# Block numbers side by side in DRAM, and tiles that travel on all 128 partitions, in a graph-network kernel

## The reference

```python
msg  = concat([h[src], h[dst]]) @ WM + bM            # one row per edge, 64 wide
s, mean_sq, mx, mn = sum, mean of squares, max, min of msg over the edges into each node
agg  = concat([mean, mx, mn, std, var, s])
hu   = concat([h, agg, agg * amp, agg * att]) @ WU + bU
hbn  = batchnorm(hu / sqrt(n))
out  = leaky_relu(hbn @ Wmix + bmix) + h
h    = relu(batchnorm(out)) + h
```

## Time and profile before

| what | value |
|---|---|
| median of three runs | 3956.39 us |
| the profiled execution, its span on the core | 3968.1 us |
| TensorE / VectorE / GpSimd busy | 84% / 79% / 56% of the span |
| DMA moved | 668.65 MB in 300094 packets |
| SP's queue (q1) | 188676 packets, 35.4% of 16 engines' span |
| fetches of numbers, keeps, fetches of one-hots | 130, 130, 395, of 593.1 KB each |

### The profile page before, as it was taken

One profiled execution on the slowest core, in us unless ns is written; L12 is line 12 of the kernel. 1 busy time (PEld: TensorE's weight loads), 2 busy tenths in 40 slices (PEclk: granted clock), 3 DMA queues, 4 the chain that ended last, 5 costly groups with the idle time before them and its releaser, 6 DMA issues.

```text
span 3968.1 us, 88783 instructions
## 1 busy us (share of the span) xinstructions
PE 3314.0 (84%) x29640; PEld 2061.9 (52%) x29640; DVE 3137.6 (79%) x6027; ACT 1168.6 (29%) x3428; POOL 2223.3 (56%) x2221
## 2 busy tenths in 40 slices
PE   0055699898887799999998699999988799999986
PEld 0022344444446657555558456555557466655575
DVE  6598588788776778888877678888876788888876
ACT  4302122222223612222225322222225332222243
POOL 6402577666654037777753147777750177777640
PEclk9997899999998899999999899999999899999997
DMA  7003799889896056556672256566670366566750
GB/s 209 16 0 81 217 257 258 239 247 254 248 258 210 14 163 178 175 173 191 201 232 77 79 157 178 170 175 191 198 240 16 118 174 180 170 189 189 219 163 34
DMA packets 300094, 668.65 MB, mean 169 GB/s; under 512 B 81751, under 2 KB 180237, under 8 KB 296995
## 3 DMA queue, kind: packets, MB, share of 16 engines
q1 hardware_dynamic: 188676, 419.32, 35.4%
q0 software_dynamic: 78400, 192.26, 18.5%
q10 hardware_dynamic: 32732, 54.15, 3.9%
HBM read 517.78 MB, written 151.72 MB: 169 GB/s over the span
## 4 chain that ended last, share of the span: by engine, by line
PE 21%; issue 20%; DMA 18%; DVE 12%; POOL 12%; ACT 2%; SPq 1%; DVEq 1%; ACTq 0%; POOLq 0%
POOL rows L881 11%; DMA rows<-table,lists 10%; PE bank L1815 8%; DMA RE<-vd 6%; PE bank L1789 4%; PE bank L1882 4%; DVE accL L1438 2%; DVE scr L1361 2%; PE bank L1798 2%; DVE scr L1372 1%; DVE accL L1434 1%; PE bank L1870 1%; DMA RE<-ohd 1%; DMA left<-accL 1%; SPq L476 1%
## 5 line engine op out<-in xcount | busy, mean ns | idle before, releaser
L881 POOL DMA_INDIRECT rows<-table,lists x1828 | 1833.0, 1003 | 836.6 <-issue 518.1
L1815 PE MATMUL bank<-RE,split 125*64 125x482 bf16 x15600 | 1846.5, 370 | 18.9 <-ACT scr L605 18.9
L1815 PEld LDWEIGHTS bank<-RE,split 125*64 125x64 bf16 x15600 | 948.9, 111 | 691.0 <-issue 34.2
L632 ACT ACTIVATE split<-rows,masks 128x128 f32<-128x128 f32 x1828 | 600.1, 391 | 1693.5 <-DMA rows<-table,lists 1311.9
L1789 PE MATMUL bank<-RE,split 126*64 126x482 bf16 x7800 | 924.2, 372 | 79.8 <-DVE scr L1372 60.4
L1361 DVE TENSOR_TENSOR scr<-scr,bank 128x964 f32<-128x964 f32 x624 | 692.1, 1109 | 78.8 <-PE bank L1789 74.0
L1372 DVE TENSOR_TENSOR scr<-scr,bank 128x964 f32<-128x964 f32 x624 | 692.0, 1109 | 45.0 <-PE bank L1798 40.0
L1789 PEld LDWEIGHTS bank<-RE,split 126*64 126x64 bf16 x7800 | 471.6, 111 | 430.5 <-DVE scr L1372 67.1
L1798 PE MATMUL bank<-RE,flip_w 126*64 126x482 bf16 x2600 | 391.4, 373 | 112.8 <-DVE scr L1361 69.0
L1433 DVE TENSOR_TENSOR accL<-accL,rows 128x192 f32<-128x192 f32 (+2 forms) x664 | 224.6, 338 | 292.8 <-DMA rows<-table,lists 289.9
L1438 DVE TENSOR_TENSOR accL<-accL,split 128x384 f32<-128x384 f32 (+2 forms) x664 | 343.1, 517 | 1.7
(11 more groups left out here) (282 smaller groups left out, 2752.9 us busy)
## 6 DMA issues: line engine op xcount, KB each, us to landing
RE<-ohd SPq DMA_DIRECT2D x395, 593.1 KB
RE<-vd SPq DMA_DIRECT2D x130, 593.1 KB
ohd<-RE SPq DMA_DIRECT2D x130, 593.1 KB
rows<-table,lists POOLq DMA_INDIRECT x1828
left<-accL POOLq DMA_DIRECT2D x20, 1280.0 KB
dense_d<-scr ACTq DMA_DIRECT2D x104, 241.0 KB
split<-dense_d ACTq DMA_DIRECT2D x16, 625.0 KB, 6.5
table<-accL SPq DMA_DIRECT2D x36, 250.0 KB
```

The source lines that it names most:

```text
L632: ins = nc.scalar.activation(masked_rows[:, g % GM_RING * GC + k, :], ring[:, b * GC + k, :], ACT.Copy, scale=masks[:, m:m + 1])
L881: nc.gpsimd.indirect_dma_start(ring[:, b * GC + k, :], None, table, bass.IndirectOffsetOnAxis(ap=lists[:, c:c + 1], axis=0)).then_inc(col_ ...
L1815: ins = nc.tensor.matmul(SB[h * D:(h + 1) * D, 0:CH], split[0:NP, k, q, h * D:(h + 1) * D], columns_of(k, NP), start=k == 0 and q == 0, st ...
```

## The change

The numbers are copied once, DRAM to DRAM, to a new array `by_chunk` in which the 2410 numbers of a chunk and group lie side by side. A fetch of numbers then is one run of 2410 for each partition. It and the keeps, the fetches of one-hots and the compare use all 128 partitions in place of 126; `ohd` grows to 128 rows a tile. TensorE's reads (126 or 125 rows) stay as they are.

```diff
-    ohd = nc.dram_tensor("ohd", (NCH * GROUPS, NP + 1, GB), BF16).ap()
+    ohd = nc.dram_tensor("ohd", (NCH * GROUPS, P, GB), BF16).ap()
     vd = nc.dram_tensor("vd", (TILES, QP), BF16).ap()
+    by_chunk = nc.dram_tensor("by_chunk", (NCH, TILES * CH), BF16).ap()
...
             sp.wait_ge(S["vd_st"], 16 * 5)
-            numbers = vd.rearrange("(g k) q -> g k q", k=RING)
+            sp.dma_start(by_chunk.rearrange("c (k n) -> c k n", n=CH), vd.rearrange("k (c n) -> c k n", n=CH)).then_inc(S["chunked"], 16)
+            sp.wait_ge(S["chunked"], 16)
+            numbers = by_chunk.rearrange("c (g n) -> (c g) n", g=GROUPS)
...
-                sp.dma_start(VB[slot][0:NP + 1, :].rearrange("p (k n) -> p k n", k=RING),
-                             numbers[g:g + 1, :, ds(c * CH, CH)].to_broadcast([NP + 1, RING, CH])).then_inc(vb_ld[slot], 16)
+                sp.dma_start(VB[slot], numbers[ds(c * GROUPS + g, 1), :].to_broadcast([P, GB])).then_inc(vb_ld[slot], 16)
...
-                sp.dma_start(ohd[ds(g, 1), :, :].rearrange("o p n -> (o p) n"), BK[b][0:NP + 1, :]).then_inc(oh_st[b], 16)
+                sp.dma_start(ohd[ds(g, 1), :, :].rearrange("o p n -> (o p) n"), BK[b]).then_inc(oh_st[b], 16)
...
-                sp.dma_start(BK[g % STREAM][0:NP + 1, :],
+                sp.dma_start(BK[g % STREAM],
                              ohd[ds(ahead, 1), :, :].rearrange("o p n -> (o p) n")).then_inc(oh_ld[g % STREAM], 16)
...
-                    nc.vector.tensor_scalar(BK[b][0:NP + 1, :], VB[g % 2][0:NP + 1, :], answers[0:NP + 1, :], None,
+                    nc.vector.tensor_scalar(BK[b], VB[g % 2], answers, None,
                                             ALU.is_equal).then_inc(S["cmp"], 1)
```

More of the change, by code:

```diff
@@ L367, in build @@
             "codes codes_ps codes_ev hot_done ps1 ps1_used ps2 rank_done sc_pos pos_ld "
-            "e_ready e_used v_ps v_int v_low v_ev vd_st cmp "
+            "e_ready e_used v_ps v_int v_low v_ev vd_st chunked cmp "
             "big_mx big_mx2 turns_done "
```

## The result

The changed kernel takes 3895.62 us (median of 4 runs, 3876.84 to 3901.81) against 3956.26 us, a ratio of 0.9833 with a 95% interval of 0.9814 to 0.9852: 61 us faster. 3868 was forecast, in a range of 3822 to 3922. Its runs spread over 25 us, those of before over 3 us. The profiled execution has a span of 3897.3 us, 71 us less than before's 3968.1.

The account below looks back on a forecast made before the run. Layer 0's dense part was taken as bound by DMA on fourteen full engines. Middle -68, start -8, end -5, layers 1 to 3 -7 and copy 0 make -88 us: 3956.4 to 3868 us, range 3822 to 3922.

Parts of the forecast that it names:

- Fourteen full engines: Layer 0's dense part: transfers of 126 rows use 14 DMA engines, which are full; 128 rows get 16.
- The middle of layer 0: Layer 0, 560 to 1200 us: pace falls from 6.32 to 5.65 us a group, gaining 68 us, bounds 22 and 107.
- the term of 5.56 for DMA: Middle of layer 0: 5.56 us a group if all DMA-bound again, two transfers of 32.2 us on 16 engines plus 1.53.
- that of 5.26 for GpSimd: Middle of layer 0: TensorE with GpSimd limit the pace to 5.26 us a group, taken from layer 1.
- The start of layer 0: Stretch up to 560 us: gain of 8 us, bounds 0 and 20; gain ahead of the gathers' lists capped at about 9.
- The copy: Start of layer 0: the new copy of 650 pieces uses 13 engines, 3.1 us plus some 2.5 to land, hidden, cost 0.
- The end of layer 0: The last compare's 13.1 us wait for numbers shrinks: gain of 5 us, bounds 0 and 13.
- Layers 1 to 3: One-hot fetches on 16 engines instead of 14, with TensorE at 98%: 7 us gain in all, bounds 0 and 30.
- The signs: Whole launch: 144 packets a transfer, compare waits under 30 us, middle pace 5.5 to 5.8, VectorE 90% or more, later layers within 5 us each.
- One address read by 128 rows: Slower rival, fetch of numbers: repeated reads of the same 4820 bytes get dearer, middle loses 42 us, 3998 us; chance 0.06.
- The faster rival: All layers: full-width transfers also faster for each engine, 24 us a transfer, pace 5.3, -134 us, 3822 us; chance 0.16.
- The gathers take over: Middle of layer 0: VectorE's waits for gathered rows keep the pace at 6.0, 3916 us; the smaller gain's chance 0.13.

Follow-up runs that it names:

- experiment 4: The changed kernel, with GpSimd leaving out the third gather of each column group in all layers (output not the reference's): 3797.20 us, ratio 0.9592.

## Why the prediction was right, and where it was off

- **Fourteen full engines.** Right. Width and run length, taken apart, each take off 0.75 us of DMA time a group, and the packet counts show 126 + 14 and 128 + 16, and 16 + 13 in place of 5 + 5 for the cut stores. The Trainium skill's rule on the number of DMA engines (DMA: Bandwidth & Descriptors, "Why a DMA increments its semaphore by 16 and not by 1") agrees, and for 125 rows too.
- **The middle of layer 0.** 68 us were forecast. The pace came out at 5.75, not 5.65, which is 101 x 0.57 = 57 us; over the same 90 groups, from the 31st to the 121st compare, it fell from 6.27 to 5.74. The number was near partly by luck, as two errors offset each other: the term of 5.56 for DMA was too high and that of 5.26 for GpSimd too low. DMA needs 4.73, because a transfer costs 28.8 us and not 32.2, and the other queues 1.13 and not 1.53. GpSimd needs (410 + 110) / 93.9 = 5.54 us a group. I had taken its limit from layer 1's pace, but that was TensorE's: the gathers of both kernels' stretches say what GpSimd itself needs (before's layer 1 at 1450 to 2050 us, then after at 560 to 1100):

```profile
L881 POOL DMA_INDIRECT rows<-table,lists x444 | 439.2, 989 | 170.8 <-issue 124.1 <-DVE accL L1438 46.6
...
L883 POOL DMA_INDIRECT rows<-table,lists x381 | 409.1, 1074 | 130.1 <-issue 110.1 <-DVE accL L1440 20.1
```

In layer 1 it was (439.2 + 124.1) / 114 = 4.94 us a group. Layer 0 has 4.06 gathers a group instead of 3.89 (its 457 gathers start at 457 us, when 14 of the 130 groups are past their compare), and each costs 1.36 us with its issue instead of 1.27. Much of the second rise goes with the compares, which run only in layer 0: in this stretch the 136 gathers that overlap a compare take 1.22 us in the mean, the other 244 take 0.99, as layer 1's do. A longer gather is likelier to overlap one, so this is a strong sign and not a proof. The Trainium skill (SBUF — State Buffer, "Who interferes with whom") has VectorE operations of this kind in a two-port mode lock GpSimd out while it writes descriptors; the durations fit, but no run here takes the compare away.
- **The start of layer 0.** Mis-sized: 8 us forecast, 0.6 seen. The step that failed was to take the gathers' lists (cap of 9 us) for the gate. The gate was ScalarE's order of issues, which held the 24.6 us won by the 13th compare until nothing was left of them; it is visible in before's trace in the same place, and I had not read that engine's rows.
- **The copy.** Right. Issued at 346.60 and landed before the next fetch's issue at 352.45, 5.8 us (5.6 forecast); the first compare starts at 367.6 (367.3 before). Cost 0. The queue from 346 to 352.4 us shows 663 packets, which are 650 pieces and 13 closing ones, so 13 engines as forecast:

```profile
q1 hardware_dynamic: 663, 0.63, 34.8%
```

- **The end of layer 0.** The last wait for numbers fell from 13.1 us to 5.9, 7 us against 5 forecast.
- **Layers 1 to 3.** 5.2 us against 7, but this is no confirmation, as the same stretch differs by more between executions with equal fetches there (2552.6 and 2563.7 us). And their bound was not TensorE alone, as experiment 4 shows.
- **The signs.** Of those named as right, two missed narrowly: VectorE is at 89.6% and not 90 in the middle of layer 0, and layer 2 is 5.6 us shorter, not within 5.
- **Rivals.** One address read by 128 rows is not slower: 28.4 us a fetch, under the 31.7 for a fetch of one-hots before. The faster rival wanted 24 us a transfer at 25 GB/s an engine; a packet got 10% cheaper, not 25%. "The gathers take over" is half of what happened, through GpSimd's time and not through landing times: VectorE's waits for gathered rows hardly moved, 43.9 us in 540 against 45.8 in 640.

On the sum: -71 us between the profiled executions where -88 was forecast; -8 is the start's, -11 the middle's, -2 the later layers', and the end gave 2 more. The median moved by 61, 10 less than the profiles, within the 25 us over which the changed kernel's runs spread.

## What to carry to other kernels

Where the mean DMA share stands near 0.9 and the consumers still wait, count packets for each transfer: here what they exceed the runs by told how many engines took part, and those were full. Every transfer of a kernel has its own row count, and with it its own number of engines (here 126 rows had 14 and 125 had 5), so look at all of them; here 52 us, nearly as much as the change's 61, lay in 14 stores a layer that it didn't touch. And when a bound is lifted, price the next engine in the same stage and from its own busy and issue time, since in another stage, without the same neighbours, its rate was too good here.

## What the runs showed that I had not expected

- Fewer and wider transfers on SP's queue made GpSimd's transfers cheaper too: its queue took 20.7% of 640 us for 397 gathers before (5.3 us of DMA time each, the writes of sums included), and 17.2% of 540 us for 381 after (3.9 us). With long runs on 126 rows it was 20.1% (4.7 us), with short runs on 128 rows 17.1% (4.1 us). So the width, more than the run length, goes with it. Why is open.
- ScalarE was held 60 us by issuing 13 stores, most of them of 250 KB, 4.6 us each. With the stores cut to more engines it took 25 us. So the issuing engine was held by its transfers, and with it what stood behind them.
- The kernel of before spread over 3 us in its first four runs and over 20 and 22 us in the nine beside each set of experiments.
